# A cross-attention and mixture-of-experts kernel: the shared feed-forward of the last two blocks of tokens is dealt out anew between attention and experts

## The reference, cut to what matters

```python
x = x + xattn(layernorm(x), ctx, ...)      # h = tanh(txt + feat + b); softmax over the 77 rows; two tanh gates
y = layernorm(x)
probs = softmax(y @ gate)                                  # 4096 tokens x 8 experts
scores, token_idx = top_k(probs.T, k=512)                  # per expert
h = gelu(y[token_idx] @ W1[e] + b1[e]);  out = (h @ W2[e] + b2[e]) * scores      # 8 experts
routed = zeros.at[token_idx].add(out)
shared = gelu(y @ Ws1 + bs1) @ Ws2 + bs2                   # all tokens
return x + routed + shared
```

## Time and profile before

| | us |
|---|---|
| median of three runs | 906.81 (905.6 to 909.69) |
| the profiled execution, whole | 906.81 |
| its span in the trace | 905.1 |
| PE busy | 803.4 (89%) |
| ACT busy | 768.1 (85%) |
| DVE busy | 712.6 (79%) |
| POOL busy | 312.5 (35%) |
| mean granted TensorE clock | 0.984 of full speed |

### The profile page before, as it was taken

The page is one execution under the profiler, slowest core; times in us unless marked ns, Lnnn a source line. Parts: engine busy times, 40 slices in busy tenths (PEclk is TensorE's granted clock), DMA queues, the critical chain, the costliest instruction groups (busy, mean ns, idle before and its releaser), DMA issues.

```text
span 905.1 us, 14088 instructions
## 1 busy us (share of the span) xinstructions
PE 803.4 (89%) x5355; PEld 471.3 (52%) x5355; DVE 712.6 (79%) x1412; ACT 768.1 (85%) x600; POOL 312.5 (35%) x563
## 2 busy tenths in 40 slices
PE   6975678568999999899999999999877999999995
PEld 4321123114343444444544445546765899999985
DVE  5799888998979698988889895985787777667640
ACT  4989999999999999999999999996651677676671
POOL 3300540536524007674101820070303144454423
PEclk9899999999999999999999999999999999999998
DMA  8000000000001000200000110003102365545512
GB/s 266 15 1 1 1 1 1 1 24 23 2 1 47 1 1 24 70 1 1 24 1 1 34 38 1 24 24 105 36 1 73 119 183 140 141 118 113 136 21 34
DMA packets 32405, 41.80 MB, mean 46 GB/s; under 512 B 2365, under 2 KB 29011, under 8 KB 32339
## 3 DMA queue, kind: packets, MB, share of 16 engines
q1 hardware_dynamic: 26083, 32.49, 10.9%
q0 software_dynamic: 6144, 8.39, 5.6%
q10 hardware_dynamic: 112, 0.04, 0.0%
HBM read 28.33 MB, written 12.58 MB: 45 GB/s over the span
## 4 chain that ended last, share of the span: by engine, by line
PE 34%; ACT 29%; issue 7%; POOL 6%; DVE 5%; ACTq 0%; DVEq 0%; POOLq 0%
ACT z L975 24%; PE bank L894 10%; PE bank L917 9%; PE bank L774 4%; PE bank L825 4%; PE bank L810 2%; ACT u L1012 2%; POOL xn L1103 2%; ACT z L971 2%; PE bank L703 1%; PE bank L932 1%; DVE z L1333 1%; ACT L1012 1%; PE bank L868 1%; DVE onehot L1609 1%
## 5 line engine op out<-in xcount | busy, mean ns | idle before, releaser
L975 ACT ACTIVATE z<-z 128x4096 f32<-128x4096 f32 (+5 forms) x157 | 520.7, 3360 | 8.6 <-DVE z L1333 8.2
L1333 DVE TENSOR_SCALAR z<-feat,txt_bias 128x1024 f32<-128x1024 f32 (+1 forms) x722 | 422.8, 656 | 21.2 <-PE bank L774 19.9
L774 PE MATMUL bank<-z,window 128*32 128x512 f32 x2464 | 308.9, 606 | 64.0 <-ACT z L975 62.5
L774 PEld LDWEIGHTS bank<-z,window 128*32 128x32 f32 x2464 | 68.7, 110 | 247.4 <-issue 138.0
L825 PE MATMUL bank<-ws_sb,u 128*128 128x256 f32 x512 | 126.0, 388 | 0.0
L825 PEld LDWEIGHTS bank<-ws_sb,u 128*128 128x128 f32 x512 | 92.3, 190 | 39.1 <-issue 28.6
L810 PE MATMUL bank<-tr,ws_s 128*128 128x512 f32 x384 | 109.1, 422 | 0.5 <-issue 0.5
L894 PE MATMUL bank<-xg_s,w_s 128*128 128x512 f32 x384 | 99.5, 397 | 0.2 <-DVE xg_s L1635 0.2
L917 PEld LDWEIGHTS bank<-w_s,hid_s 128*128 128x128 f32 x672 | 86.3, 188 | 4.0
L810 PEld LDWEIGHTS bank<-tr,ws_s 128*128 128x128 f32 x384 | 71.1, 193 | 32.9 <-issue 19.6
L917 PE MATMUL bank<-w_s,hid_s 128*128 128x256 f32 x672 | 88.2, 280 | 0.0
(11 more groups left out here) (237 smaller groups left out, 783.3 us busy)
## 6 DMA issues: line engine op xcount, KB each, us to landing
w_raw<-in_L_ffn_W_dram SPq DMA_DIRECT2D x16, 1024.0 KB, 5.7
x_ring<-in_x_dram SPq DMA_DIRECT2D x8, 512.0 KB, 8.5
xn_dram<-xn SPq DMA_DIRECT2D x8, 512.0 KB, 2.9
out_dram<-x_ring SPq DMA_DIRECT2D x8, 512.0 KB, 2.9
u<-in_L_ffn_Ws_dram SPq DMA_DIRECT2D x1, 1024.0 KB, 11.2
ws_sb<-in_L_ffn_Ws_dram SPq DMA_DIRECT2D x1, 1024.0 KB, 13.6
xg<-xn_dram,idx POOLq DMA_INDIRECT x32, 4.1
out_dram<-y,idx POOLq DMA_INDIRECT x32, 3.9
```

The source lines that it names most:

```text
L774: ins = e.matmul(sums[v][32 * r:32 * r + 32, :], window[:, c, 31 - k:63 - k], z[:, n % ZB, at_piece:at_piece + TOK], start=(v, r) not in b ...
L975: e.activation(part, part, ACT.Tanh).then_inc(signal(*step), 1)
L1333: ins = e.tensor_scalar(z[:, n % ZB, i * width:(i + 1) * width], feat_of(units, c), bias_of(units, t, c), None, ALU.add)
```

## The change

It deals out the seam's filler anew, moves a few steps and adds one.

- Block 6: before, its slices 0 and 1 were finished early (`up` 0 to 3, `gelu` 0 to 3 one at a time in gaps of ACT, `down` of slices 0 and 1 before `probs_turn`, `up` 4 and 5 behind it). Now only `up` 0 to 3 stand ahead of the search. Their four `gelu` stand together behind `logits_exp` and `router` of block 7, and the first `down` in round 0.
- A new step `keep` on PE behind `up` 3 of block 6: eight matmuls of the identity with itself, 128 columns each, whose result nobody reads.
- The two `down_end` of block 5, before in the chain ahead of `weigh` and behind `gates`, now stand behind `probs_turn`, ahead of `digits`. The two of block 6 move from round 7 to behind `ranks`. The two of block 7 move from ahead of `listed` of expert 1 to behind the second `e_lo` of expert 0.
- Block 7's slices begin behind round 9 instead of in round 5.
- `split_lo` of `w2` for expert 0 moves from behind `g_lo` to ahead of `mark` of expert 1.
- `mark` of expert 1 waits until the second of the four gathers of expert 0 has landed. The four `mark_slots` of expert 1 then stand together, and so do its four `list`.
- The first `e_up` of an expert waits for both `g_lo` before its first matmul, instead of for each part where it is read.

```diff
-TAIL_FILL = (4, 3)
-GELUS_BEFORE = 1
+TAIL_FILL = (4, 0)
+KEEP = 8
-TEST_FILL = (2, 4, 2, 2, 2, 2, 0, 4, 2, 0)
-RANK_FILL = (2, 2, 3, 2)
-EXPERT_FILL = (10, 5, 1)
-SECOND_FILL = (3, 1, 2, 2, 5)
-LIST_FILL = (1, 0, 0, 0)
+TEST_FILL = (2, 4, 3, 2, 1, 2, 1, 3, 2, 0)
+RANK_FILL = (2, 3, 3, 1)
+EXPERT_FILL = (5, 6, 1)
+SECOND_FILL = (5, 6, 1)
+LIST_FILL = (1, 2, 0, 1)
...
-    filler = begun(va) + last_ffn[:ENDS_BEHIND] + [down_ends(va)] + last_ffn[ENDS_BEHIND:] + [down_ends(vb)]
+    filler = late_ffn(va, 4) + last_ffn[:ENDS_BEHIND] + [down_ends(va)] + last_ffn[ENDS_BEHIND:] + [down_ends(vb)]
...
-    fill_chain(4)
-    ends = [step for step in lead if step[0] in BY_VECTOR]
-    order += [*ends[:1], *held[:GELUS_BEFORE], *end[4], *end[5], *ends[1:], *end[6], *held[GELUS_BEFORE:]]
+    fill_chain(TAIL_FILL[0])
+    order += [("keep",), *end[4], *end[5], *end[6], *end[7], *end[9], *end[8], ("logits_exp", vb), ("router", vb),
+              ("values", NT - 2 * J, NT), *held, ("probs_turn",)]
     held.clear()
-    order += [*end[7], *end[9], *end[8], ("logits_exp", vb), ("router", vb), ("values", NT - 2 * J, NT)]
     order += [step for step in lead if step[0] == "down" and step[1:3] in late]
-    fill_chain(TAIL_FILL[0])
-    order.append(("probs_turn",))
+    order += [step for step in lead if step[0] in BY_VECTOR]
     fill_chain(TAIL_FILL[1])
...
-    low = [("split_lo", *step[1:]) for step in first_split]
-    order += low[:PIECES[0]]
+    order += [("split_lo", *step[1:]) for step in first_split]
     fill(SECOND_FILL[0])
-    order.append(("mark", 1))
-    for q in range(4):
-        order += [("mark_slots", 1, q), ("list", 1, q)]
-        fill(SECOND_FILL[1 + q])
-    order += [("listed", 1), ("fold", 1), ("folded", 1), ("gather", 1)]
-
+    order += [("mark", 1), *(("mark_slots", 1, q) for q in range(4))]
+    fill(SECOND_FILL[1])
+    order += [*(("list", 1, q) for q in range(4)), ("listed", 1)]
+    fill(SECOND_FILL[2])
+    order += [("fold", 1), ("folded", 1), ("gather", 1)]
...
-    order += turn_gathered(0) + low[PIECES[0]:]
+    order += turn_gathered(0)
...
+                elif kind == "keep":
+
+                    e.wait_ge(bank_empty[MISC[1]], used[MISC[1]])
+                    for _ in range(KEEP):
+                        ins = e.matmul(banks[MISC[1]][:, 0:P], ident[:], ident[:], start=True, stop=True)
+                    ins.then_inc(signal(*step), 1)
...
                     if m == 0:
+                        e.wait_ge(*done("g_lo", ex, 0))
+                        e.wait_ge(*done("g_lo", ex, C - 1))
...
-                            if m == 0 and n < 2:
-                                e.wait_ge(*done(("g_hi", "g_lo")[n], ex, c))
...
+                    if ex == 1:
+                        e.wait_ge(first_gathered[1], 16)
```

## The result

The changed kernel took 915.9 us in the median (913.06 to 917.63, six runs) against 907.02 (905.6 to 909.69, six runs) for the kernel before: ratio 1.0091, 95% interval 1.007 to 1.0112. It is slower by 8.9 us in the medians, and by 8.1 between the two profiled executions, where 2 were forecast. The profiled execution of after took 914.94 us, its span is 913.2 us against 905.1, and PE, ACT and DVE were busy about as long as before.

The account below looks back on a forecast made before the run. The prediction took the PE-bound experts as fixed behind the seam, a race of the chain against PE's filler. Second `fold` at 699.85 against 698.35, plus 0.55, made +2.05: 908.9 us against 906.81, range 904.5 to 912.5.

Parts of the forecast that it names:

- The bound: PE fills the experts at full clock, so the run ends a fixed time after the first `e_up` has its operands.
- Part 1: Seam up to round 0: `total` of round 0 at 640.6 instead of 641.76, a gain of 1.1 us.
- The rival that asked for a drain of 1.4 us: ACT's table load ahead of round 0 also costs a drain: 1.4 us on top, 910.3 us; chance 0.05.
- Parts 2 and 3: Clock falls ahead of round 0, 1.95 us lost, perhaps again in round 4, 1.0 more; `total` 9 then at 670.4.
- Part 4: Ranking and expert 0's list: first `fold` 16.2 us after `total` 9, before 14.0.
- Part 5: First to second `fold`: 13.25 us instead of 14.88, 1.6 gained; the new wait on the second gather costs 0 to 0.6.
- Part 6: Second `fold` to experts: waiting for both `g_lo` delays the first `e_up` by 0.55 us, bounds 0.2 to 0.9.
- The transfers moved ... hides them: Between the folds: expert 1's loads and block 6's store go out between gathers; rows needed 7 us later, which hides them.
- a third fall of the clock: Rival: the clock drops once more at the first `e_up`, costing 1.9 us, giving 910.8 us; chance 0.10.
- The rival of a clock that stays low through round 1: Rounds 0 and 1 then lose 4.9 us instead of 1.95; with round 2, 6.5: 911.8 to 913.5 us; chance 0.12.
- PE idle at the four `list`: Sign against the forecast, at expert 1's `list`: it would mean the marks and not the filler are last.
- a wait on the gather longer than 1 us: Sign against the forecast, between the folds, where the wait of `mark` was put at 0 to 0.6 us.

Follow-up runs that it names:

- n3: The changed kernel with 29 identity matmuls spread over the gap ahead of round 0 instead of 8 at its front: 910.92 us, ratio 1.0027 to before.
- n6: n5 with 12 more identity matmuls in round 4: 906.84 us, ratio 0.9996 to before.
- n1: The changed kernel without the wait of expert 1's `mark` on the second gather: 910.72 us, ratio 1.0029 to before.
- n2: The changed kernel, wait kept, with expert 1's two weight loads issued only when expert 0's fourth gather has landed: 911.34 us, ratio 1.0033 to before.
- n10: n6 with the first `e_up` again waiting for each part where it is read: 905.69 us, ratio 0.9966 to before.
- n8: The changed kernel without the wait on the gather, the first `e_up` again waiting part by part: 908.08 us, ratio 1.0002 to before.
- n4: The kernel before with only the wait of expert 1's `mark` on the second gather added: 915.48 us, ratio 1.0089 to before.
- n5: The changed kernel with the edits of n1 and n3 together: 907.27 us, ratio 0.9996 to before.
- n11: n7 with ten identity matmuls added behind `total` of round 6: 904.83 us, ratio 0.9945 to before.
- n12: The changed kernel measured once more, with no edit: 914.8 us, ratio 1.0061 to before.
- n7: The kernel before with its filler pieces moved ahead of expert 1's `mark`: 903.62 us, ratio 0.9954 to before.
- n9: n7 with expert 1's two weight loads issued only when the fourth gather has landed: 903.93 us, ratio 0.9945 to before.

## Why the prediction was wrong, step by step

- **The bound** held: from the first bias matmul of expert 0 on, nothing changed. That matmul is 8.13 us later in after than in before, and the spans differ by 8.1 us.
- **Part 1** was nearly right: `total` 0 at 641.11 against 640.6. The second half of `y_turn` waits for a bank that `low_digits` (DVE, L1489) reads, and that step, in round 0 in both kernels, now stands behind the two moved `down_end` (the 2.48 in the timeline above). But the miss is the clock: `y_turn` began at 640.16 in after and at 640.12 in n3, where it took 0.63 us instead of 1.09, and `total` of round 0 came at 640.61, the forecast. That these transposes would run at the low clock was left out of the sum. One table load is left; ACT in after:

```profile
635.17 1.28 ACT L1001 ACT_TABLE_LOAD   x1
636.46 2.42 ACT L1001 ACTIVATE u<-bank,vec 128x512 f32<-128x512 f32 x4
```

The load ends at 636.45 and the first `gelu` begins at 636.46. The rival that asked for a drain of 1.4 us, after the Trainium skill ("ScalarE: Activation LUTs", What ACT_TABLE_LOAD costs), does not show here: the ACT instruction ahead of the load ended at 635.15, 0.02 us before it, so there is no such gap on either side. Round 0 goes by the row.

- **Parts 2 and 3** held in mechanism: the clock fell ahead of round 0 (low from 638.3 to 645.1) and again in round 4 (658.8 to 665.6). `total` 1 came at 645.57 (forecast 645.15), 5 at 660.38 (659.4), 9 at 671.69 (670.4): 1.3 late. n3 showed the first low clock to be worth 2.3 at round 1, not 1.95, and n6 the second 1.2, where I had 1.0.
- **Part 4** held: 15.79 from `total` 9 to `fold`, forecast 16.2.
- **Part 5 is the step that failed.** Forecast 13.25 from `fold` to `fold`, measured 17.65. I let the second gather land 6.5 after the `fold`; its issue was where I put it (3.06 behind, forecast 2.96), but it took 6.81 us where I had 3.5, so `mark` started 9.9 after. The wait on it, which I had at 0 to 0.6, was 4.01. The marks so ended 15.65 after the `fold` instead of 12.1, and behind them came the low clock: the last half of `down` took 2.08, in n1 at full clock 1.13. The 3.5 was the median of eight gathers, four of them expert 1's, of which the first took 2.7. The gather in question has its own row in the trace of before. The transfer issued at 686.43, in the view of transfers (count, us to landing):

```profile
xg<-xn_dram,idx POOLq DMA_INDIRECT x1, 6.3
```

With 6.3 in place of 3.5 the marks of Part 5 would have started 2.8 us later. The rest of the part was sound: without the wait (n1) the `fold`s are 12.80 apart, and with a quick gather (n2) 13.65, against my 13.25. "The transfers moved ... hides them" was the same mistake from the other side: I asked whether the loads are in time, not what they do to the gathers beside them.

- **Part 6** was mis-sized: 1.35 more than before (7.78 against 6.43), forecast 0.55, bounds 0.2 to 0.9. The wait for both parts is worth 0.8 (n10 against n6) to 1.2 (n8 against n1). In after the eight transposes in this stretch also ran partly at the low clock, 1.63 us where n1 had 1.06; how the rest divides is open.

The terms add up: 1.3 − 0.4 + 4.4 + 0.8 is 6.1 over a forecast of 2.05, which is the 8.1 measured. Of the rivals, a third fall of the clock came, but at the four `list` and because of the wait. At the first `e_up` the clock was low in n4, n5, n11 and n12, in no trace of before or n1. The rival of a clock that stays low through round 1 did not come, and its price was added wrongly: `total` of round 2 at 640.6 + 13.7 = 654.3 is 4.9 later than the 649.4 of the forecast, which makes 913.8 and not 911.8. "PE idle at the four `list`" and "a wait on the gather longer than 1 us" stood as signs that would make the forecast wrong, and both were there. The result lies above the range by 3.4 us, and without the 4.4 of Part 5 it would lie within it: the wait's bounds, 0 to 0.6, came from a single, mixed landing time.

## What to carry to other kernels

Price a wait on a transfer by the landing time of that very transfer, in the traffic it will be in, and not by a median over its group; and look at which load is issued beside it. Where an engine is made to wait, add what the engines fed by it lose, here PE's clock. Filler that stands where its engine is already behind can be moved forward into idle time (n7), until another wait, here the last gather, is the one that ends last. Matmuls that compute nothing can bring back what a lost clock costs (n3, n6), but did not where another wait took the gain (n11).

## What the runs showed of the hardware

- A gather of 128 rows landed in 2.7 to 3.7 us with no load beside it (n2, n9). With a 1 MB load issued 0.44 us behind it, it took 5.64 (n4), 6.3 (before), 6.81 (after) and 6.91 us (n12).
- About the same idle time can leave the clock full or bring it down: 2.77 us in before and 2.78 in n4 left it, 2.78 in n7 did not; 2.92 in after brought it down, 2.92 at the same place of the same kernel in n12 did not.
- The three low stretches in after lasted 6.8, 6.8 and 3.4 us. Counted from the next filler or `list`, as the forecast counted, they ended 4.0 (645.1 against 641.17), 5.2 and 3.3 us on, within the 3.1 to 5.7 seen in before; in n4 it was 5.3. Only n12's was longer, 10.2 us, over a stretch in which PE had small pieces with waits between them.
- Matmuls of the identity held the clock as 29, spread over the gap (n3), and did not as a burst of eight, 1.95 us long, at its front (after). Their number and their places changed together, so which of the two counts was not separated.
